# Mixing all 32 batches' expert weights together in 64-row halves, a quarter of the inner width at a time

## The reference

```python
h = relu(einsum('bsh,oh->bso', x, gate_w1) + gate_b1)
g = (einsum('bso,eo->bse', h, gate_w2) + gate_b2).mean(axis=1)   # [32, 8]
mW1 = W1 + einsum('be,efh->bfh', g, TW1)                         # [32, 512, 128]
mb1 = b1 + g @ Tb1
mW2 = W2 + einsum('be,ehf->bhf', g, TW2)                         # [32, 128, 512]
mb2 = b2 + g @ Tb2
u = gelu(einsum('bsh,bfh->bsf', x, mW1) + mb1[:, None, :])
out = einsum('bsf,bhf->bsh', u, mW2) + mb2[:, None, :]
# and around it: h = layernorm(x) * (1 + cb) + sb; x = x + gb * out
```

## Time and profile before

| | us |
|---|---|
| median of 3 runs | 707.73 (706.77 to 708.25) |
| the profiled execution, its own time | 707.83 |
| its span | 705.8 |
| TensorE busy, share of the span | 94% |
| VectorE, ScalarE, GpSimd busy | 77%, 54%, 31% |
| first layer matmul of the expert part starts at | 532.1 |

### The profile page before, as it was taken

How to read it: one execution, slowest core, us unless ns; L and a number is a source line. 1 busy time by engine, 2 the same in 40 slices (tenths; PEclk the granted TensorE clock), 3 DMA queues, 4 the chain that set the end, 5 groups by cost and what they waited for, 6 DMA issues and landing times.

```text
span 705.8 us, 24615 instructions
## 1 busy us (share of the span) xinstructions
PE 662.1 (94%) x9075; PEld 510.5 (72%) x9075; DVE 542.2 (77%) x1242; ACT 382.0 (54%) x907; POOL 217.5 (31%) x351
## 2 busy tenths in 40 slices
PE   4697999999999999999999999999869999999998
PEld 3365677667776677776677766677569899998996
DVE  5777898999998999989999989998747255472552
ACT  2264566567766677765677665777522423324232
POOL 3344444345533345443445343454320000000000
PEclk9999999999999999999999999999979999999999
DMA  3666410110011100101100101100500010000001
GB/s 105 169 84 85 57 31 22 30 30 22 22 30 24 35 22 22 30 22 28 31 22 22 30 22 31 29 15 22 68 2 2 25 37 7 30 22 30 30 8 52
DMA packets 65797, 24.84 MB, mean 35 GB/s; under 512 B 38440, under 2 KB 64360, under 8 KB 65648
## 3 DMA queue, kind: packets, MB, share of 16 engines
q1 hardware_dynamic: 64320, 18.25, 10.8%
q0 software_dynamic: 1456, 6.31, 6.0%
HBM read 16.13 MB, written 8.40 MB: 35 GB/s over the span
## 4 chain that ended last, share of the span: by engine, by line
PE 77%; DVE 17%; issue 4%; ACT 1%; DMA 0%; POOL 0%; DVEq 0%; SPq 0%; ACTq 0%; POOLq 0%
PE SB L822 8%; PE WB L810 8%; PE SB L889 7%; DVE rden L639 7%; PE WB L975 7%; PE WB L921 5%; PE WB L940 4%; PE WB L797 4%; PE WB L925 4%; PE SB L797 4%; DVE mx L553 4%; DVE Pr L560 3%; PE SB L1036 3%; PE WB L849 3%; PE WB L837 2%
## 5 line engine op out<-in xcount | busy, mean ns | idle before, releaser
L390 ACT ACTIVATE Pr<-Pr 128x512 f32<-128x512 f32 x128 | 77.9, 639 | 130.6 <-DVE Pr L560 130.6
L498 ACT ACTIVATE Pr<-WB,mb1T 128x256 f32<-128x256 f32 x128 | 49.9, 478 | 75.5 <-PE WB L810 75.5
L560 DVE TENSOR_TENSOR Pr<-SB,mx 128x512 f32<-128x512 f32 x128 | 84.6, 681 | 3.6
L553 DVE TENSOR_REDUCE mx<-SB 128x8 f32<-128x512 f32 x128 | 84.4, 680 | 3.7 <-PE SB L874 3.7
L395 ACT COPY PT<-SB 128x512 f32<-128x512 f32 x128 | 75.3, 591 | 4.3 <-PE SB L889 3.6
L364 POOL TENSOR_TENSOR attT<-a_gated,rem_g 128x256 f32<-128x256 f32 x32 | 23.2, 725 | 172.1 <-DVE a_gated L654 172.1
L639 DVE RECIPROCAL rden<-WB 128x256 f32<-128x256 f32 x32 | 56.2, 1758 | 21.8 <-PE WB L925 21.8
L335 POOL TENSOR_TENSOR KM<-K_ch,bd_scale 128x1024 f32<-128x1024 f32 x32 | 60.6, 1895 | 38.0 <-ACT K_ch L407 38.0
L889 PE MATMUL SB<-ident,Pr 128*128 128x128 f32 x512 | 66.9, 273 | 1.1 <-ACT Pr L390 1.0
L975 PE MATMUL WB<-GKBD,GQT 128*128 128x512 f32 (+1 forms) x128 | 56.4, 524 | 8.1 <-DVE wait_carrier L740 4.5
L889 PEld LDWEIGHTS SB<-ident,Pr 128*128 128x128 f32 x512 | 58.8, 141 | 5.2 <-ACT Pr L390 1.4
(11 more groups left out here) (188 smaller groups left out, 1416.8 us busy)
## 6 DMA issues: line engine op xcount, KB each, us to landing
x_all<-in_L_attn_x SPq DMA_DIRECT2D x32, 128.0 KB, 2.1
v_rows<-V_rows SPq DMA_DIRECT2D x32, 128.0 KB, 1.8
VBD<-v_rows SPq DMA_DIRECT2D x128, 32.0 KB, 1.9
TW<-in_L_ffn_TW POOLq DMA_DIRECT2D x16, 256.0 KB, 10.0
GA<-ga_rows POOLq DMA_DIRECT2D x1, 2048.0 KB, 12.8
out_x<-attT SPq DMA_DIRECT2D x16, 128.0 KB, 1.8
out_x<-y_ga SPq DMA_DIRECT2D x16, 128.0 KB, 1.8
PT<-in_L_ffn_W SPq DMA_DIRECT2D x2, 256.0 KB
```

Of the source, the lines that this page charges most:

```text
L390: nc.scalar.activation(Pr[:, k, :], Pr[:, k, :], ACT.Exp).then_inc(p_ready, 1)
L553: nc.vector.tensor_reduce(mx[:, k, :], SB[k][:].rearrange("p (h j) -> p h j", h=8), AX.X, ALU.max).then_inc(mx_ready, 1)
L560: nc.vector.tensor_tensor(Pr[:, k, :].rearrange("p (w h c) -> p h w c", w=2, h=8), SB[k][:].rearrange("p (h w c) -> p h w c", w=2, h=8), b ...
```

## The change

All 32 batches are mixed together, and the inner width of 512 is taken in 4 quarters (`FC`): for each quarter c, first the 128 inner rows of W1 for all batches, then the first layer of all batches, the 128 inner columns of W2 for all batches, and the second layer of all batches.

- **Halves.** J is 8 instead of 16: 8 experts by 8 rows are 64 rows, and TW1 and TW2 lie in SBUF as two halves of 64 rows that hold alternate groups of 8 rows of the weight. A mixing matmul has 64 rows and 32 batches by 8 rows = 256 columns; the two halves (`r`) write to different banks. `mix(c, part, kk)` issues four matmuls, two for each half. A quarter has 8 such calls, four for W1 and four for W2.
- **Order.** TensorE's mixing calls of W2 stand behind every second pair of batches in the first half of the first layer; those of the next quarter's W1 stand between the last four pairs of the second layer. All loops are written out.
- **Rows.** `mixed_rows` adds 512 elements as before; the output has runs of 8 floats.
- **Second layer.** Each quarter's product of a batch goes to PSUM on its own. For the first quarter ScalarE writes it to an accumulator in SBUF, times the block's gate and plus the bias (`begin_sum`); for the other three VectorE adds it (`add_chunk`, scalar_tensor_tensor). The 32 accumulators of 256 floats lie in tiles of the attention part. After the last quarter `final_T` transposes, VectorE adds x in place, two batches at a time, and SP stores 256 KB in each of 16 DMAs.
- **Gates.** `experts` runs for 28 batches after step 33 and for the last 4 after step 35. No mixing stands in the pipeline's last steps.
- **Loads.** `load_experts` issues four DMAs for an expert, of half the size, instead of two.

```diff
-    J = P // E
-    GB = 8
-    NG = B // GB
+    J = HALF // E
+    B0 = B - 4
+    NPAIR = B // 2
...
             def load_experts(e):
-                pool.dma_start(TW1[J * e:J * e + J], ins["L0_ffn_TW1"][e].rearrange("(i j) h -> j i h", j=J)
-                               ).then_inc(tw_loaded, 16)
-                pool.dma_start(TW2[J * e:J * e + J], ins["L0_ffn_TW2"][e].rearrange("(i j) f -> j i f", j=J)
-                               ).then_inc(tw_loaded, 16)
+                for r in range(2):
+                    rows = slice(HALF * r + J * e, HALF * r + J * e + J)
+                    pool.dma_start(TW1[rows], ins["L0_ffn_TW1"][e].rearrange("(i r j) h -> r j i h", r=2, j=J)[r]
+                                   ).then_inc(tw_loaded, 16)
+                    pool.dma_start(TW2[rows], ins["L0_ffn_TW2"][e].rearrange("(k r j) f -> r j k f", r=2, j=J)[r]
+                                   ).then_inc(tw_loaded, 16)
...
+            def begin_sum(p):
+                act.wait_ge(ffn2_done, p + 1)
+                for k in range(2):
+                    b = 2 * p + k
+                    nc.scalar.activation(acc[b], WB[2 + p % 2][:, k * S:(k + 1) * S], ACT.Identity,
+                                         scale=gbT[:, b:b + 1], bias=gmb2T[:, b:b + 1]).then_inc(acc_begun, 1)
...
+            def mixed_rows(c, part, kk, r):
+
+                dve.wait_ge(mix_done, 16 * c + 8 * part + 2 * kk + r + 1)
+                rows = slice(4 * J * kk, 4 * J * (kk + 1))
+                dst, base = (mW2, W2T[:, c, :]) if part else (mW1[:], W1T[:, c * P:(c + 1) * P])
+                nc.vector.tensor_tensor(dst[:, :, rows].rearrange("p b (k r j) -> p r k b j", k=2, r=2)[:, r],
+                                        SB[(2 * kk + r) % 4][:].rearrange("p (k b j) -> p k b j", k=2, b=B),
+                                        bc(base[:, rows].rearrange("p (k r j) -> p r k j", k=2, r=2)[:, r], [P, 2, B, J], 2),
+                                        ALU.add).then_inc(mixed, 1)
...
+            def add_chunk(c, p):
+                n = c * NPAIR + p
+                dve.wait_ge(ffn2_done, n + 1)
...
+                for k in range(2):
+                    b = 2 * p + k
+                    nc.vector.scalar_tensor_tensor(acc[b], WB[2 + n % 2][:, k * S:(k + 1) * S], gbT[:, b:b + 1], acc[b],
+                                                   ALU.mult, ALU.add).then_inc(acc_added, 1)
...
+            def mix(c, part, kk):
+
+                for r in range(2):
+                    n = 16 * c + 8 * part + 2 * kk + r
+                    if n >= 4:
+                        pe.wait_ge(mixed, n - 3)
+                for k in range(2 * kk, 2 * kk + 2):
+                    for r in range(2):
+                        rows = slice(HALF * r, HALF * r + HALF)
+                        lhsT = TW2[rows, k, c * P:(c + 1) * P] if part else TW1[rows, c * J + k, :]
+                        last = mm(SB[(2 * kk + r) % 4][:, (k % 2) * S:(k % 2 + 1) * S], lhsT,
+                                  Gd[rows].rearrange("p b j -> p (b j)"), start=True, stop=True)
+                        if k % 2 == 1:
+                            last.then_inc(mix_done, 1)
...
+            pe.wait_ge(tw_loaded, N_TW)
+            pe.wait_ge(g_ready, N_G0 + 2)
+            for kk in range(4):
+                mix(0, 0, kk)
+            pe.wait_ge(g_ready, N_G)
+            for c in range(FC):
+                for p in range(8):
+                    ffn1(c, p)
+                    if p % 2 == 0:
+                        mix(c, 1, p // 2)
+                for p in range(8):
+                    for q in (2 * p, 2 * p + 1) if p < 4 else (p + 4,):
+                        ffn2(c, q)
+                        if c == FC - 1 and q >= 2:
+                            final_T(q - 2)
+                    ffn1(c, 8 + p)
+                for kk in range(4):
+                    ffn2(c, 12 + kk)
+                    if c + 1 < FC:
+                        mix(c + 1, 0, kk)
+                    else:
+                        final_T(10 + kk)
```

More of the change, by code:

```diff
@@ L290, in _ @@
             step(B)
[L292 to L298, removed]
+            for p in range(NPAIR):
+                sp.wait_ge(o_ready, p + 1)
+                sp.dma_start(out[2 * p:2 * p + 2].rearrange("b (t p) d -> p (b t) d", p=P),
+                             x_all[:, 2 * p * S:(2 * p + 2) * S].rearrange("p (t d) -> p t d", d=D)).then_inc(stored, 16)
+            sp.wait_ge(stored, 16 * NPAIR)
         @block.gpsimd
@@ L776, in _ @@
+            for p in range(NPAIR - 2, NPAIR):
+                out_rows(p)
         @block.tensor
@@ L787, in _ @@
             mm(WB[2][0:B, 0:D], siluT[:], wmod[:, 2 * D:3 * D], start=True, stop=True).then_inc(mod_done, 1)
-            def mix(g, m):
-                for k in range(4):
-                    if m < 8:
-                        lhsT = TW1[:, 4 * m + k, :]
-                    else:
-                        c, half = divmod(m - 8, 2)
-                        lhsT = TW2[:, 4 * half + k, c * P:(c + 1) * P]
-                    last = mm((WB if m < 8 else SB)[m % 4][:, k * P:(k + 1) * P], lhsT,
-                              Gd[:, bass.ds(g * (J * GB), J * GB)], start=True, stop=True)
-                last.then_inc(mix_done, 1)
@@ new lines, in ffn1, with ffn2 @@
+            def ffn1(c, p):
+                n = c * NPAIR + p
+                if p == 0:
+                    pe.wait_ge(mixed, 16 * c + 8)
+                if n >= 2:
+                    pe.wait_ge(gelu_done, 2 * (n - 1))
+                for k in range(2):
+                    b = 2 * p + k
+                    last = mm(WB[n % 2][:, k * S:(k + 1) * S], mW1[:, b, :], h2T[:, b * S:(b + 1) * S], start=True, stop=True)
+                last.then_inc(ffn1_done, 1)
+            def ffn2(c, p):
+                n = c * NPAIR + p
+                if p == 0:
+                    pe.wait_ge(mixed, 16 * c + 16)
+                if 2 <= n < NPAIR + 2:
+                    pe.wait_ge(acc_begun, 2 * (n - 1))
+                elif n >= NPAIR + 2:
+                    pe.wait_ge(acc_added, 2 * (n - 1) - B)
+                pe.wait_ge(gelu_done, 2 * (n + 1))
+                for k in range(2):
+                    b = 2 * p + k
+                    last = mm(WB[2 + n % 2][:, k * S:(k + 1) * S], mW2[:, b, :], u[b % 16], start=True, stop=True)
+                last.then_inc(ffn2_done, 1)
@@ L831, in final_T @@
+            def final_T(p):
+                pe.wait_ge(acc_added, B * (FC - 2) + 2 * (p + 1))
+                pe.wait_ge(mixed, 16 * FC)
+                if p >= 4:
+                    pe.wait_ge(o_ready, p - 3)
+                for k in range(2):
+                    for t in range(T):
+                        last = nc.tensor.transpose(SB[p % 4][:, (2 * k + t) * P:(2 * k + t + 1) * P],
+                                                   acc[2 * p + k][:, t * P:(t + 1) * P], ident[:])
                 last.then_inc(fin_done, 1)
@@ L1027, in step @@
                     gates(it)
-                if isinstance(it, int) and it == B + 3:
-                    for m in range(2, 4):
-                        mix(0, m)
                 if has(it, 4):
```

236 lines of the change are left out of this document (88 added, 148 removed).

## The result

| | before | the change |
|---|---|---|
| median | 707.99 (706.77 to 708.73) | 732.98 (731.66 to 733.87, 4 runs) |
| ratio, 95% interval | | 1.0343 [1.0322, 1.0363] |
| span of the profiled execution | 705.8 | 732.1 |
| hidden matmul of batch 30 starts at | 520.65 | 550.63 |
| from there to the end | 185.2 | 181.5 |

A forecast was written before the change was run, and what follows sets the result against it. The prediction took TensorE to bound the expert stage, without idle time there. Its terms, -25.8 + 10.6 + 6.05 - 1.45 + 7.6 + 1.4 + 4.8 = +3.2 us on 707.83, gave 711.0 us, range 701 to 721.

The forecast's parts named there:

- POOL's queue: Expert weight loads: 32 half-size DMAs instead of 16 keep POOL issuing longer and delay work queued behind: +4.8 us.
- fully exposed, twice: After attention steps 2 and 3, POOL's extra issuing of +2.0 us each delays KM and GKBD, for which TensorE waits.
- Mixing in halves: Expert stage: two half-row mixing matmuls overlap fully on TensorE, 24.2 us inside the stage instead of 50.0: -25.8 us.
- the changes of shape: Expert stage: TensorE switches between full and half rows 56 times at 0.19 us each: +10.6 us.
- rival of cheap changes: TensorE's shape changes cost nothing and POOL's half-sized issues cost half: 699 us, chance 0.22.
- that of no overlap: Rival: the half-row mixing matmuls do not run together, so mixing costs 55 us: 738 us, chance 0.06.
- The start: Expert stage's beginning: nothing mixes before all 32 gates, so the first layer matmul comes later: +6.05 us, with -1.45 for bias matmuls.
- VectorE's rows: Additions of 512 elements after mixing: output in runs of 8 floats takes 0.65 us a row, before 0.92.
- the bound: Rival: VectorE's rows stay at 0.93 us and VectorE bounds the stage: +8.7, 719.7 us, chance 0.12.
- New waits: Expert stage: TensorE waits for VectorE's rows at each quarter's layers, gelu's table load and the last quarter: +7.6 us net.
- the 1.2 us of the last quarter: Part of TensorE's waits: in the last quarter VectorE (0.88 + 0.65 a step) lags TensorE (1.30): 1.2 us.
- The end: After the last transposes: two output additions of 512 and a last store of 256 KB instead of 128: +1.4 us.

The follow-up runs named there:

- run 1: The kernel before, with each expert load cut in two by SBUF rows (32 DMAs of 8 rows, 128 KB each), nothing else changed: 735.38 us, ratio 1.0384.
- run 2: The kernel before, with each expert load cut in two by columns (32 DMAs of 16 rows, 128 KB each): 714.99 us, ratio 1.0096.
- run 5: The change, with its expert loads issued half an expert (two DMAs) in each of POOL's steps 4 to 19: 699.72 us, ratio 0.9881.
- run 3: The kernel before, with its expert loads spread, one expert in each of POOL's steps 4 to 11: 701.7 us, ratio 0.9907.
- run 9: The change with loads over steps 4 to 19, paired mixing calls, first W1 mixed early, last four batches' small matmuls behind the tenth pair: 691.28 us.
- run 4: The change, with its expert loads spread, four DMAs in each of POOL's steps 4 to 11: 717.06 us, ratio 1.0126.

## Why the prediction was wrong, step by step

- **POOL's queue (+4.8, bounds 0 and 6.5), the step that failed.** "Issuing one occupies POOL for 0.53 to 0.66 us, almost whatever its descriptors" and "fully exposed, twice" were right: the two waits for GKBD grew by 3.2 us and the one in the drain by 1.3, 4.5 together. (Eight issues took 4.9 us, not 4.3; the earlier trace rows give 4.8.) The step priced the issue of a load and never the load. Moved from 16 rows to 8 it lands in twice the time (13.9 against 6.9 us at the same size and count), and while it drained TensorE stood still in the steps that are written out, by my reading for its own instructions. That is 25.5 us that no term of the sum had: 21.7 of stalls and 3.8 that remained, at the halved clock. It is more than the 22.0 us between 711.0 and 732.98, mainly since the expert stage came out 2.1 us better than forecast. The Trainium skill (DMA: Bandwidth & Descriptors, Why a DMA increments its semaphore by 16 and not by 1) says that a DMA is spread over the largest number of engines, up to 16, that divides the slowest dimension of both its sides, so one load of 8 rows would use 8 of 16. No record here tells which engine carried a packet, and the rows show that half the engines is not the whole reason: in the windows of the stalls q0 kept 57.9% and 61.7% of all 16 busy, more than half. What did grow is the time in packets: for the same bytes q0's packets took 9.9% of the engines' span in run 1 and 5.8% in run 2. Why they take longer stays open. A sign of it was in the trace before too: the stall of 1.67 us with no releaser in the scores, which the forecast did not ask about.
- **Mixing in halves (-25.8) and the changes of shape (+10.6): right.** 0.21 and 0.19 us a change where 0.19 was taken, and full overlap. The rival of cheap changes is refuted; so is that of no overlap. A change back to full rows costs about as much as one into halves.
- **The start (+6.05): near.** The first layer matmul came 12.76 us after batch 31's hidden matmul (554.61 to 567.37), where the forecast had 13.55. Counted from batch 30's hidden matmul it came 5.25 us later than in the kernel before (16.74 against 11.49), where 6.05 was taken.
- **VectorE's rows: right.** 32 rows take 20.6 us, 0.64 each (before, 0.92); 0.65 was taken. VectorE was not the bound.
- **New waits (+7.6): too high by some 2 us.** Each quarter's first layer waited 1.4 us, not 1.6 to 1.8, and the second layer 0.3, not 0.6; the 1.2 us of the last quarter did not come (0.3 ahead of one transpose).
- **The end (+1.4): right.** From the last transposes to the end of the span it was 3.4 us, and is 4.9.
- **Their sum.** A gain of 1.6 us was forecast for all but POOL. With the sizes measured (0.20 for each of 56 changes, 5.25, waits of 5.4 net, 1.5) the sum is 3.9; the traces say 3.7, and the medians of run 5 and run 3 say 2.0.

That the change is slower, as forecast, is luck: the reason given was that the side costs eat up the gain in mixing, and in the traces they left 3.7 us of it. With the loads out of the way the same expert stage is some 2 to 3 us faster than before, and the sign of the change turns, by an amount that the ratios alone do not quite resolve.

## What to carry to other kernels

A change of layout changes the transfers that fill it. Price a DMA three times: the time to issue it, the time to land, and what others on the same engines (small transfers in a dependency chain, and by my reading instructions in code that is written out) have to wait while it runs; a stall with "issue" as releaser in the middle of one matmul's passes was the sign of the third here. When a slow result sits in a stage whose arithmetic was not touched, put the change's side effects alone into the old kernel first: run 1 showed the whole loss with one edited function and no other part of the change. And where a shape change costs a fixed 0.2 us, longer blocks buy it back (6.8 us here); the version of run 9, 691.28 us, is 2.5% faster than the kernel before, of which spreading the loads alone gives 0.9%.

## What the runs showed of the hardware that was not expected

- Loads of the same size and number landed in 13.9 us onto 8 rows and 6.9 us onto 16 rows, and their queue's packets took 9.9% and 5.8% of the engines' span. With only two of the 8-row loads a step they landed in 6.9 us.
- 8-row loads, four a step, slow others: 32 KB transfers of SP took 8.8 us in place of 1.9. Two a step: 6.3 us, hidden.
- TensorE lost 7.6 to 8.4 us at a time in the change, up to 6.1 in run 1 and 1.67 in the kernel before, in code that is written out; in the change each stall ended 2 to 3 us behind a packet of q8 that came as the weight loads ran out. In run 4, with the same loads beside the loop, the score passes stood still for 0.3 us in all.
- Thirty-two passes of 32 columns took 1.98 us, as long as 16 passes of 256 columns.
